# State-space layer: the gate's projection as wide tiles ahead of the loop, products and outputs in twos, tokens weighed ahead of convolutions 4 and 5

## The chip, the cores and the metric

The program runs on one core of a Trainium2 chip. It is a decoder of twelve sublayers on 8 sequences of 128 tokens with 256 channels each; it runs as one launch. The time is device time in microseconds. The kernel before took 2154.83 us (median of three executions, 2151.45 to 2156.3). The change touches the first sublayer alone, a state-space layer that takes about a quarter of the span.

## The reference, cut to what matters

The layer has 32 heads; each has 64 channels of x, 128 of b and 128 of c, and 64 of a gate z. In the reference's terms, for an input of 8 x 128 x 256:

```python
z, x, b, c, dt = split(x @ Win.T)             # per head: 64, 64, 128, 128, 1
x, b, c = (silu(causal_conv(u, w, taps=4)) for u in (x, b, c))
dt  = softplus(dt + dt_bias)
cum = cumsum(-exp(A_log) * dt, over tokens)
y[t] = sum over s <= t of (c[t] . b[s]) * exp(cum[t] - cum[s]) * dt[s] * x[s]
y   = y * silu(z), scaled by the norm of y in each head, then Wout
```

The kernel computes the recurrence as products inside one sequence (128 x 128 for each head and sequence), which is what the sum above says.

## The kernel before, in words

The tokens of all 8 sequences are the free axis (T = 1024), channels are the partitions. `state_space(p)` has three blocks, with a barrier of all engines between them.

The first block (L1702 to L1756) projects dt for all heads on TensorE (L1713), makes softplus and the decays on VectorE (L1732 to L1741), has TensorE sum them over time (L1718), and has VectorE split the sums in three bf16 parts (L1751 to L1756). VectorE also splits the layer's input in a rounded part `XT_hi` and a rest `XT_lo` (L1746, L1747). SyncE starts the load of the next sublayer's weights (L344).

The second block is a loop over 16 pairs of heads, written as a first step, a loop of seven trips with two steps each, and two last steps. One step works on two pairs at once: "a" is the pair whose inputs are projected and convolved, "b" is the pair before it, whose products are made. A pair has five tiles of 128 channels (x, two of b, two of c); I call them 1 to 5, in the code they are 0 to 4.

- Projection of a tile (`project`, L1855): 12 matmuls of 512 columns, in three terms of rounded parts (weights high by input high, high by rest, rest by high) so that the fast 4-byte type keeps the precision. GpSimd makes the two parts of the weights (L1812, L1813). The tiles use two pairs of PSUM banks in turn, so the projection of tile k+2 waits for the convolution of tile k.
- Tap (`tap`, L1960, ScalarE): the last tap of the convolution, from PSUM. Convolution (`convolve`, L2024, VectorE): the three other taps, three dependent instructions. Then `silu` (L1969, ScalarE).
- `turn_x` (L1903, TensorE): tile 1 transposed in two halves; `weigh_x` (L2042, VectorE): each half times dt. They share bank 7.
- For pair b: `decay_sums` (L1866 to L1870, TensorE) and `decay` (L1975, ScalarE, Exp) in four groups; `products` (L1888, TensorE), `mix` (L2034, VectorE: product times decay), `outputs` (L1897, TensorE), each also in four groups, which I call 1 to 4.
- The gate: `project_z` (L1877) makes 16 matmuls of plain float32 with 128 columns each per pair; `silu` of it is L1990; its weights are the last third of the second load of the pair.
- The end of a step: ScalarE copies the outputs (L2002) and squares them (L2004), VectorE sums the squares per head (L2071), GpSimd multiplies by the gate (L1832). The next `decay_sums` wait for the square, since they write the banks that it reads.

Every engine runs its own instructions in the order written. Inside a step the order of these calls in each engine's `step` function is the schedule, and semaphores hold an engine at an instruction until its inputs or its buffer are ready; whatever is written behind waits too. The third block scales, transposes and projects the result.

## Time and profile before

| | us |
|---|---|
| median of three executions | 2154.83 (2151.45 to 2156.3) |
| profiled execution: its own time | 2158.32 |
| profiled execution: its span | 2156.5 |
| TensorE matmul busy, share of the span | 1645.3, 76% |
| VectorE busy | 1434.9, 67% |
| ScalarE busy | 728.7, 34% |
| GpSimd busy | 476.9, 22% |
| mean granted TensorE clock | 0.854 |

The span runs from the first to the last instruction; the execution's own time is 1.82 us longer. PE is TensorE's matmuls, PEld its weight loads, DVE is VectorE, ACT is ScalarE, POOL is GpSimd, SP is SyncE. A granted clock of 1.00 is 2.4 GHz and 0.50 is 1.2 GHz. The trace counts a plain float32 matmul twice (x32 for 16), and its matmul ends are modelled, so that the distance between two starts is a better length than the duration of one. Some matmul records are missing. Times in the rows are from the span's start.

### The profile page before, as it was taken

The numbers are of one execution on the slowest core, as the hardware profiler recorded it, in microseconds if no ns is written. First come the engines' busy times: TensorE is split into PE (matmuls) and PEld (weight loads), VectorE is DVE, ScalarE is ACT, GpSimd is POOL, SyncE is SP. The second block draws the span as 40 slices with busy tenths as digits, with TensorE's granted clock in tenths as the row PEclk, the third lists the DMA queues.
The fourth block names the chain that finished last, engine by engine and source line by source line (L and its number), as shares of the span: only waits on it lengthen the run. The fifth ranks groups of instructions, "written<-read, shape, count | busy, mean of one in ns | idle before, by whom it ended". The sixth has DMA issues, their size and how long they took to land. (4 is left out here: it accounts for less than half of the span.)

```text
span 2156.5 us, 32415 instructions
## 1 busy us (share of the span) xinstructions
PE 1645.3 (76%) x11633; PEld 1226.8 (57%) x11662; DVE 1434.9 (67%) x2376; ACT 728.7 (34%) x1143; POOL 476.9 (22%) x549
## 2 busy tenths in 40 slices
PE   2799999998886888166747458889995988888353
PEld 2687888887773564022446234677764875556221
DVE  3588777877225754899576673554446993677977
ACT  0466556665221441233224111333331002345111
POOL 0233323332000421277112002210001322143000
PEclk9899999999897786588869667999996997999555
DMA  2000000000000000000100002000002210100000
GB/s 106 25 24 21 29 29 29 28 16 23 0 0 21 2 7 32 0 0 0 42 3 2 25 0 100 2 19 1 1 1 64 73 39 27 51 4 2 1 0 20
DMA packets 13206, 46.80 MB, mean 22 GB/s; under 512 B 1715, under 2 KB 2356, under 8 KB 11830
## 3 DMA queue, kind: packets, MB, share of 16 engines
q1 hardware_dynamic: 13110, 45.49, 6.1%
q8 instruction: 64, 1.05, 0.2%
q14 instruction: 32, 0.26, 0.0%
HBM read 44.43 MB, written 1.05 MB: 21 GB/s over the span
## 5 line engine op out<-in xcount | busy, mean ns | idle before, releaser
L2024 DVE SCALAR_TENSOR_TENSOR arena<-psum,arena 128x1016 f32<-128x1016 f32 (+2 forms) x240 | 303.9, 1267 | 100.2 <-ACT arena L1960 94.5
L859 DVE TENSOR_REDUCE limits<-psum 128x4 f32<-128x512 f32 (+2 forms) x256 | 148.3, 620 | 95.2 <-PE psum L719 59.0
L1855 PE MATMUL psum<-ssm_XT_hi,ssm_split 128*128 128x512 f32 x640 | 196.0, 409 | 17.3 <-POOL ssm_split L1813 10.9
L827 ACT ACTIVATE PT<-psum 128x1024 f32<-128x1024 f32 x112 | 108.6, 1021 | 120.5 <-PE psum L750 120.5
L719 PE MATMUL psum<-K,QR 32*128 32x256 f32 (+1 forms) x320 | 125.0, 475 | 26.6 <-POOL K L695 16.4
L1960 ACT ACTIVATE arena<-psum,arena 128x1024 f32<-128x1024 f32 x80 | 89.0, 1112 | 158.3 <-PE psum L1855 158.3
L1855 PEld LDWEIGHTS psum<-ssm_XT_hi,ssm_split 128*128 128x128 f32 x640 | 117.4, 193 | 39.5 <-POOL ssm_split L1813 14.0
L2370 PE MATMUL psum<-expert,x 128*128 128x256 f16 x1024 | 114.7, 277 | 16.8 <-POOL expert L2356 16.8
L1812 POOL TENSOR_TENSOR ssm_split<-arena,const 128x256 fp32r<-128x256 f32 x80 | 58.4, 730 | 291.0 <-DMA arena<-in_ssm_in 164.3
L2508 POOL TENSOR_TENSOR fed<-dtx,b_all 128x1024 f32<-128x1024 f32 x32 | 103.1, 3243 | 77.8 <-ACT b_all L2557 44.3
L2370 PEld LDWEIGHTS psum<-expert,x 128*128 128x128 f16 x1024 | 101.5, 99 | 29.8 <-issue 16.9
L2383 DVE SCALAR_TENSOR_TENSOR acc<-psum,gate_now,acc 128x256 f32<-128x256 f32 x256 | 111.2, 483 | 9.2 <-PE psum L2370 8.3
L2577 DVE TENSOR_TENSOR_SCAN state<-decay,fed 128x1024 f32<-128x1024 f32 x32 | 103.1, 3262 | 6.8 <-POOL fed L2508 5.2
L1855 PE MATMUL psum<-ssm_XT_lo,ssm_split 128*128 128x512 f32 x320 | 101.5, 399 | 0.0
L719 PEld LDWEIGHTS psum<-K,QR 32*128 32x128 f32 x320 | 61.0, 219 | 58.5 <-DVE limits L859 21.2
L2521 PE MATMUL psum<-bc_parts,selector 96*128 96x512 bf16 x64 | 22.2, 479 | 89.3 <-DVE read L2585 56.0
L738 PE MATMUL psum<-Q,KT 32*128 32x256 f32 (+1 forms) x640 | 82.0, 557 | 0.4
L470 PE MATMUL psum<-const,X 128*128 128x128 f32 x176 | 41.2, 396 | 51.2 <-DVE X L514 51.2
L1897 PEld LDWEIGHTS psum<-arena,X 128*128 128x128 f32 x512 | 63.5, 191 | 23.7 <-DVE X L2034 20.8
L1897 PE MATMUL psum<-arena,X 128*128 128x64 f32 x512 | 65.9, 272 | 13.4 <-DVE X L2034 13.4
L601 PE MATMUL psum<-XT,arena 128*128 128x512 f32 x128 | 65.5, 676 | 12.9 <-PEq L885 10.0
L766 PE MATMUL psum<-PT,V 128*32 128x128 f32 x2048 | 72.5, 289 | 2.6 <-DVE O L853 2.6
(415 smaller groups left out, 3691.9 us busy)
## 6 DMA issues: line engine op xcount, KB each, us to landing
arena<-in_ssm_in SPq DMA_DIRECT2D x32, 384.0 KB, 3.1
expert_mask<-in_expert_masks SPq DMA_DIRECT2D x32, 256.0 KB, 2.6
arena<-in_L_xattn SPq DMA_DIRECT2D x1, 5120.0 KB, 15.1
arena<-in_L_ffn SPq DMA_DIRECT2D x1, 2592.0 KB, 9.1
arena<-in_L_xattn SPq DMA_DIRECT2D x2, 1280.0 KB, 5.4
arena<-in_L_attn SPq DMA_DIRECT2D x1, 2272.0 KB
arena<-in_L_ffn SPq DMA_DIRECT2D x1, 2176.0 KB, 8.5
arena<-in_L_xattn SPq DMA_DIRECT2D x1, 1667.0 KB, 6.8
```

The lines of the kernel that those rows point to most:

```text
L719: ins = nc.tensor.matmul(score_bank(r)[:, k * n:(k + 1) * n], QR[group(r), b % 2, c0 + k, :], K1[group(r), b % 2, c0 + k, :, :].rearrange( ...
L738: nc.tensor.matmul(exponents[r][:, k * n:(k + 1) * n], KT[group(r), c0 + k, b * P:(b + 1) * P], Q1[group(r), b % 2, c0 + k, :, :].rearrang ...
L827: nc.scalar.activation(PT[:, u % 2, 2 * k:2 * k + 2, :, :].rearrange("p r h q -> p (r h q)"), p.psum[:, (2 + 2 * k) * 512:(4 + 2 * k) * 51 ...
L859: ins = nc.vector.tensor_reduce(limits[:, u % 2, r, :, k], score_bank(r)[:, :].rearrange("p (h k) -> p h k", h=4)[:, :, lo:hi], AX.X, ALU. ...
L1855: ins = nc.tensor.matmul(bank[tile_bank(r, tile) + half][:, :], w_part(tile, kw, c), x_part(kx, c, slice(half * 512, (half + 1) * 512)), s ...
L1897: ins = nc.tensor.matmul(y_of(b, head), decays[:, g, q * P:(q + 1) * P], dtx[:, 1 - r, b, head * 64:(head + 1) * 64], start=True, stop=True)
L1960: nc.scalar.activation(conv[:, (r + tile) % 2, :], tile_psum(r, tile), ACT.Copy, scale=tap_now[:, r, tile, TAPS - 1:TAPS]).then_inc(s.tap_ ...
L2024: ins = nc.vector.scalar_tensor_tensor(out[:, :, ago:], product[:, :, :P - ago], tap, out[:, :, ago:], ALU.mult, ALU.add)
L2370: ins = nc.tensor.matmul(bank[b][:, :D], x16[:, part, c, b * P:(b + 1) * P], expert[:, r % 2, c, :], start=(part == 0 and c == 0), stop=(p ...
L2383: nc.vector.scalar_tensor_tensor(acc[:, b, :], bank[b][:, :D], gate[:, r % 2, b:b + 1], acc[:, b, :], ALU.mult, ALU.add).then_inc(s.produc ...
L2508: nc.gpsimd.tensor_tensor(fed[:, c, :], dtx[:, c, :], b_all[:, r, :], ALU.mult).then_inc(s.input_ready.up(trips), 1)
L2577: nc.vector.tensor_tensor_scan(state[:, c, :], decay[:, c, :], fed[:, c, :], 0.0, ALU.mult, ALU.add).then_inc(s.state_ready.up(trips), 1)
```

## The change

The gate's projection leaves the loop. Four weight tiles of 512 gate channels (`ssm_z`, 512 KB each) are loaded at the start of the first block; GpSimd splits each in two parts of 128 x 1024; TensorE makes 32 groups of six matmuls with 512 columns (three terms by two halves of the channels, the input's parts as the stationary operand) in four banks in turn, 16 groups before the cumulative sums of the decays and 16 behind; ScalarE puts the Silu of each group into `gated`. The input's split moves to the head of the block, its high part to ScalarE. In the loop the second load of a pair is 256 KB in place of 384 KB and waits for another signal. The order of the step changes on TensorE, ScalarE and VectorE: products, mixes and outputs come in twos, the products have one bank more, and the transposition of tile 1 comes behind outputs 3 and 4.

```diff
@@ first block
-            with nc.Block(no_gpsimd_drain=True) as block:
+            with ExitStack() as first, nc.Block(no_gpsimd_drain=True) as block:
+                z_split = [[first.enter_context(nc.sbuf_tensor(f"ssm_z{r}{k}", [P, T], F32R)) for k in range(2)] for r in range(2)]
+                z_raw = [gated[:, 12 + g, :] for g in range(4)]
+                z_bank = lambda n: bank[4 + n % 4]
                 @block.sync
+                    for g in range(4):
+                        sync.dma_start(z_raw[g].rearrange("p (c n) -> p c n", c=DC), p.dram["ssm_z"][g]).then_inc(s.loaded.up(16), 16)
                     p.load_next(sync)
+                @block.gpsimd
+                    for g in range(4):
+                        if g == 0:
+                            pool.wait_ge(s.loaded.sem, s.loaded.at(63))
+                        if g >= 2:
+                            pool.wait_ge(s.z_psum.sem, s.z_psum.at(8 * (g - 2) + 7))
+                        hi, lo = (a[:, :] for a in z_split[g % 2])
+                        p.pool_chain.then(pool, nc.gpsimd.tensor_tensor(hi..., z_raw[g]..., ones8, ALU.mult))
+                        nc.gpsimd.tensor_tensor(lo, z_raw[g], hi.bitcast(F32), ALU.subtract).then_inc(s.split_ready.up(), 1)
                 @block.tensor
+                    def project_z(g, b):
+                        n = 8 * g + b
+                        if b == 0:
+                            pe.wait_ge(s.split_ready.sem, s.split_ready.at(g))
+                        if n == 0:
+                            pe.wait_ge(s.x_ready.sem, s.x_ready.at(1))
+                        if n >= 4:
+                            pe.wait_ge(s.z_ready.sem, s.z_ready.at(n - 4))
+                        products = [(kw, kx, c) for kw, kx in ((0, 0), (0, 1), (1, 0)) for c in range(DC)]
+                        for kw, kx, c in products:
+                            ins = nc.tensor.matmul(z_bank(n)[:, :], (XT_hi, XT_lo)[kx][:, c, b * P:(b + 1) * P],
+                                                   z_split[g % 2][kw]...[:, c, :], ...)
+                        ins.then_inc(s.z_psum.up(), 1)
                     ...                                  # dt's projection
+                    for n in range(16):
+                        project_z(n // 8, n % 8)
                     pe.wait_ge(s.dt_ready.sem, s.dt_ready.at(0))
                     ...                                  # sums over time
+                    for n in range(16, 32):
+                        project_z(n // 8, n % 8)
                 @block.scalar
+                    nc.scalar.copy(XT_hi[:, :, :], p.XT[:, :, :]).then_inc(s.x_ready.up(), 1)
                     ...
+                    for n in range(32):
+                        g, b = divmod(n, 8)
+                        act.wait_ge(s.z_psum.sem, s.z_psum.at(n))
+                        nc.scalar.activation(gated[:, 4 * g:4 * g + 4, b * P:(b + 1) * P], z_bank(n)..., ACT.Silu).then_inc(s.z_ready.up(), 1)
@@ loop, SyncE and GpSimd
-                                sync.wait_ge(s.z_psum.sem, s.z_psum.at(m + -1))
+                                sync.wait_ge(s.split_ready.sem, s.split_ready.at(m * TILES + -1))
-                            pool.wait_ge(s.z_ready.sem, s.z_ready.at(m + -1))
@@ loop, TensorE
-                product_bank = lambda g: bank[5] if g < 2 else bank[6]
+                product_bank = lambda g: bank[(5, 6, 7, 6)[g]]
-                            pe.wait_ge(s.mixed_ready.sem, s.mixed_ready.at(n + -1))
+                            if g == 3:
+                                pe.wait_ge(s.mixed_ready.sem, s.mixed_ready.at(n + -2))
                             products(0)
-                            pe.wait_ge(weights_here[1].sem, weights_here[1].at(m * 16 + -1))
-                            project_z()
-                            outputs(0)
                             products(1)
                         if has_a:
                             project(m, r, 2)
                         if has_b:
+                            outputs(0)
                             outputs(1)
-                            pe.wait_ge(s.z_ready.sem, s.z_ready.at(m + -1))
                             products(2)
+                            products(3)
                         if has_a:
-                            pe.wait_ge(s.conv_silu.sem, s.conv_silu.at(m * TILES))
-                            turn_x(0)
                             project(m, r, 3)
                         if has_b:
                             outputs(2)
-                            products(3)
+                            outputs(3)
                         if has_a:
+                            pe.wait_ge(s.conv_silu.sem, s.conv_silu.at(m * TILES))
+                            turn_x(0)
+                            project(m, r, 4)
                             pe.wait_ge(s.dtx_ready.sem, s.dtx_ready.at(m * 2))
                             turn_x(1)
-                            project(m, r, 4)
-                        if has_b:
-                            outputs(3)
```

On VectorE, in a step of the loop, the mixes (TENSOR_TENSOR X), the convolutions (three SCALAR_TENSOR_TENSOR) and the two weighings (TENSOR_TENSOR arena, 128x512) stand so before, from mix 2 to the second weighing:

```order
L2034 TENSOR_TENSOR X<-psum,X 128x512
...
L2024 SCALAR_TENSOR_TENSOR arena<-psum,arena 128x8x127
...
L2034 TENSOR_TENSOR X<-psum,X 128x512
...
L2042 TENSOR_TENSOR arena<-psum,arena 128x512
...
L2024 SCALAR_TENSOR_TENSOR arena<-psum,arena 128x8x127
...
L2034 TENSOR_TENSOR X<-psum,X 128x512
...
L2042 TENSOR_TENSOR arena<-psum,arena 128x512
```

and in the changed kernel from mix 2 on (of each convolution the first of its three instructions is shown in both):

```order
L2066 TENSOR_TENSOR X<-psum,X 128x512
...
L2056 SCALAR_TENSOR_TENSOR arena<-psum,arena 128x8x127
...
L2056 SCALAR_TENSOR_TENSOR arena<-psum,arena 128x8x127
...
L2066 TENSOR_TENSOR X<-psum,X 128x512
...
L2066 TENSOR_TENSOR X<-psum,X 128x512
...
L2074 TENSOR_TENSOR arena<-psum,arena 128x512
...
L2056 SCALAR_TENSOR_TENSOR arena<-psum,arena 128x8x127
...
L2074 TENSOR_TENSOR arena<-psum,arena 128x512
```

Mix 2 now stands ahead of convolution 2 and mix 4 ahead of the first weighing; convolutions 2 and 3 stand together.

On TensorE, in the same step, behind outputs 2 (L1897, 128x64), stand products (L1888), the first half of the transposition (L1903, from `sin`) and the projection of tile 4 (L1855) before:

```order
L1897 MATMUL psum<-arena,X 128x64 x4
L1932 REGISTER_ALU
L1888 MATMUL psum<-ssm_bc 128x128 x4
L1903 MATMUL psum<-const,sin 128x128 x4
L1850 REGISTER_ALU
L1855 MATMUL psum<-ssm_XT_hi,ssm_split 128x512 x2
```

and in the changed kernel, from products 3 and 4 (L1929) over the projection of tile 4 (L1903, five rows) to the transposition (L1944) and the projection of tile 5:

```order
L1929 MATMUL psum<-ssm_bc 128x128 x4
L1929 MATMUL psum<-arena,ssm_bc 128x128 x4
...
L1903 MATMUL psum<-ssm_XT_hi,ssm_split 128x512 x2
L1903 MATMUL psum<-ssm_XT_lo,ssm_split 128x512 x2
L1903 MATMUL psum<-ssm_XT_hi,ssm_split 128x512 x4
...
L1938 MATMUL psum<-arena,X 128x64 x8
L1944 MATMUL psum<-const,sin 128x128 x4
...
L1903 MATMUL psum<-ssm_XT_hi,ssm_split 128x512 x2
```

The transposition that the first weighing needs moved from ahead of the projection of tile 4 to behind outputs 3 and 4.

On ScalarE, in the same step, from the first tap behind the Silu of tile 1 on, stand the taps (L1960), the Silus (L1969; L1990 for the gate), the copy (L2002) and the square (L2004) before:

```order
L1960 ACTIVATE arena<-psum,arena 128x1024
...
L1990 ACTIVATE ssm_gated<-psum 128x1024
L1969 ACTIVATE ssm_bc<-arena 128x1024
...
L1960 ACTIVATE arena<-psum,arena 128x1024
...
L1960 ACTIVATE arena<-psum,arena 128x1024
L1969 ACTIVATE ssm_bc<-arena 128x1024
...
L1960 ACTIVATE arena<-psum,arena 128x1024
L1969 ACTIVATE ssm_bc<-arena 128x1024
...
L2002 COPY ctxT<-psum 128x1024
L2004 ACTIVATE cos<-psum 128x1024
```

and in the changed kernel (taps L1996, Silus L2005, copy L2031, square L2033):

```order
L1996 ACTIVATE arena<-psum,arena 128x1024
...
L1996 ACTIVATE arena<-psum,arena 128x1024
L2005 ACTIVATE ssm_bc<-arena 128x1024 x2
...
L1996 ACTIVATE arena<-psum,arena 128x1024
...
L2031 COPY ctxT<-psum 128x1024
L2033 ACTIVATE cos<-psum 128x1024
L2005 ACTIVATE ssm_bc<-arena 128x1024
...
L1996 ACTIVATE arena<-psum,arena 128x1024
```

Tap 5, which stood ahead of the Silu of tile 4, now stands behind it; copy and square moved ahead of both.

## Rows read from the trace of the kernel before

**Rows 1.** Stretch, us, busy us (instructions) of PE, PEld, DVE, ACT, POOL, clock, DMA.

```profile
90.00:506.00 416.00, 394.58 (x2601) 338.68 (x2611) 328.28 (x307) 249.14 (x265) 134.54 (x180) 1.00 0.08 27
...
41.00:45.00 4.00, 3.32 (x16) 3.11 (x16) 3.97 (x6) 0.00 (x0) 0.00 (x0) 1.00 0.00 0
55.30:61.00 5.70, 5.62 (x13) 4.46 (x14) 0.00 (x0) 0.04 (x1) 2.85 (x5) 0.50 0.19 69
```

**Rows 2.** TensorE in order of time, one step: start us, us, engine line op, [idle before].

```profile
238.58 0.38 PE L1867 MATMUL psum<-ssm_cumT,ssm_third 96*128 96x512 bf16 x1 [0.74 <-ACT cos L2004]
...
241.00 0.71 PE L1855 MATMUL psum<-ssm_XT_hi,ssm_split 128*128 128x512 f32 x2
...
243.82 1.12 PE L1888 MATMUL psum<-ssm_bc 128*128 128x128 f32 x8
244.78 3.74 PE L1877 MATMUL psum<-arena,XT 128*128 128x128 f32 x32
248.35 1.00 PE L1897 MATMUL psum<-arena,X 128*128 128x64 f32 x8
249.19 1.11 PE L1888 MATMUL psum<-arena,ssm_bc 128*128 128x128 f32 x8
...
254.66 0.60 PE L1903 MATMUL psum<-const,sin 128*128 128x128 f32 x4
```

**Rows 3.** VectorE in order of time, the same step.

```profile
258.61 0.68 DVE L2042 TENSOR_TENSOR arena<-psum,arena 128x512 f32<-128x512 f32 x1
259.21 3.87 DVE L2024 SCALAR_TENSOR_TENSOR arena<-psum,arena 128x1016 f32<-128x1016 f32 x3
262.99 0.68 DVE L2034 TENSOR_TENSOR X<-psum,X 128x512 f32<-128x512 f32 x1
...
268.97 1.21 DVE L2071 TENSOR_REDUCE arena<-cos 128x1024 f32 x1
```

**Rows 4.** ScalarE in order of time, the same step.

```profile
244.33 1.28 ACT L1969 ACT_TABLE_LOAD   x1 [0.60 <-DVE arena L2024]
...
246.59 1.10 ACT L1960 ACTIVATE arena<-psum,arena 128x1024 f32<-128x1024 f32 x1
...
264.03 1.12 ACT L1960 ACTIVATE arena<-psum,arena 128x1024 f32<-128x1024 f32 x1 [3.92 <-PE psum L1855]
```

**Rows 5.** VectorE in order of time: the sums of squares, first, fifteenth and last.

```profile
119.89 1.21 DVE L2071 TENSOR_REDUCE arena<-cos 128x1024 f32 x1
...
537.45 1.21 DVE L2071 TENSOR_REDUCE arena<-cos 128x16 f32<-128x1024 f32 x1
...
560.05 1.22 DVE L2071 TENSOR_REDUCE arena<-cos 128x16 f32<-128x1024 f32 x1 [3.17 <-ACT cos L2004]
```

**Rows 6.** All engines in order of time, the layer's first block.

```profile
26.25 7.01 PE L1713 MATMUL psum<-arena,XT 128*128 128x32 f32 x32 [0.97 <-PEq L391]
...
41.12 3.32 PE L1718 MATMUL psum<-const,ssm_bc 128*96 128x128 f32 x16 [7.86 <-DVE ssm_bc L1741]
...
49.78 0.68 DVE L1756 CAST ssm_cumT<-ssm_bc 32x1024 bf16<-32x1024 f32 x1
...
55.38 1.22 PE L1855 MATMUL psum<-ssm_XT_hi,ssm_split 128*128 128x512 f32 x2 [10.94 <-POOL ssm_split L1813]
```

**Rows 7.** DMA issues: out<-in engine op xcount, KB each, us to landing.

```profile
arena<-in_L_xattn SPq DMA_DIRECT2D x2, 1280.0 KB, 5.4
...
arena<-in_L_ffn SPq DMA_DIRECT2D x1, 2176.0 KB, 8.5
```

**Rows 8.** GpSimd by line: out<-in xcount | busy us, mean ns | idle before.

```profile
L2508 POOL TENSOR_TENSOR fed<-dtx,b_all 128x1024 f32<-128x1024 f32 x32 | 103.1, 3243 | 77.8 <-ACT b_all L2557 44.3 <-DVE state L2577 33.4
...
L1832 POOL TENSOR_TENSOR ssm_gated<-ctxT,ssm_gated 128x1024 f32 x14 | 33.1, 2363 | 21.8 <-ACT ctxT L2002 21.8
L695 POOL TENSOR_TENSOR K<-KT,const 128x512 fp32r<-128x512 f32 x32 | 32.6, 1040 | 0.0
```

**Rows 9.** ScalarE by line, the same columns.

```profile
L1975 ACT ACTIVATE X<-psum 128x512 f32<-128x512 f32 x64 | 33.2, 604 | 0.5 <-PE psum L1870 0.3
```

More of the change, by code:

```diff
@@ L1683, in state_space @@
             dtx = spare(2, B, P)
-            bc = [[spare(T) if (r, k) == (1, 3) else sb2(f"bc{r}{k}", [P, T])[:, :] for k in range(TILES - 1)] for r in range(2)]
+            early = [sb2(f"bc0{k}", [P, T])[:, :] for k in range(2)]
+            late = spare(T)
             XT_hi = sb2("XT_hi", [P, DC, T], F32R)
@@ L1689, in state_space @@
             third = sb2("third", [P, 2, SSM_H], BF16)
-            dta3 = bc[0][0][:, :B * 3 * SSM_H].rearrange("p (b k h) -> p b k h", b=B, k=3)
-            rest = bc[0][1]
+            dta3 = early[0][:, :B * 3 * SSM_H].rearrange("p (b k h) -> p b k h", b=B, k=3)
+            rest = early[1]
             ones = p.c("ones").rearrange("p (o n) -> p o n", o=1).broadcast_to([P, DC, P])
@@ L1757, in state_space @@
             p.close()
+            bc = [early + [sb2(f"bc0{k}", [P, T])[:, :] for k in (2, 3)], [sb2(f"bc1{k}", [P, T])[:, :] for k in range(3)] + [late]]
             def steps(engine, emit, chain=None, links=0):
@@ L1871, in decay_sums @@
                             ins.then_inc(s.decay_psum.up(trips), 1)
-                        def project_z():
-                            for b in range(B):
-                                for c in range(DC):
-                                    ins = nc.tensor.matmul(bank[6 + b // 4][:, b % 4 * P:(b % 4 + 1) * P], p.XT[:, c, b * P:(b + 1) * P],
-                                                           raw[:, 1, c, 2 * P:], start=(c == 0), stop=(c == DC - 1))
-                            ins.then_inc(s.z_psum.up(trips), 1)
                         def products(g):
                             n = m * 4 + (g - 4)
-                            pe.wait_ge(s.mixed_ready.sem, s.mixed_ready.at(n + -1))
+                            if g == 3:
+                                pe.wait_ge(s.mixed_ready.sem, s.mixed_ready.at(n + -2))
                             for q in range(4):
@@ L2004, in step @@
                             nc.scalar.activation(square[:, :], p.psum[:, 4 * 512:6 * 512], ACT.Square).then_inc(s.square_ready.up(trips), 1)
+                        if has_a:
+                            silu(m, r, 3)
+                            tap(m, r, 4)
                         if has_next:
@@ L2060, in step @@
                             mix(2)
+                            mix(3)
                         if has_a:
@@ L2063, in step @@
                             convolve(m, r, 3)
-                        if has_b:
-                            mix(3)
-                        if has_a:
                             weigh_x(1)
```

45 lines of the change are left out of this document (23 added, 22 removed).

## The prediction, made before the changed kernel ran

> **What bounds the kernel now.** I read the windows first, then one step of the loop engine by engine, then the layer's first block. In the loop TensorE is busy 394.58 of 416 us (95%) and VectorE 328.28 (79%) [rows 1]; the reader is to see that TensorE looks full but that VectorE is not far behind. The sums of squares, one per step, stand 29.83 us apart: (537.45 - 119.89) / 14 [rows 5]. So the loop has one fixed period, and the question is which circle of waits closes in it.
>
> One step, read off starts [rows 2]: the four decay sums take 2.64 (241.00 - 238.58, and 0.22 for their first matmul, whose record is missing), a projection 2.82 (243.82 - 241.00), one group of products 0.96, the gate's projection 3.57 (248.35 - 244.78), one group of outputs 0.84. On VectorE a convolution holds the engine 3.78 and is done after 3.87, a mix or a weighing 0.60 (0.68), the sum of squares 1.13 (270.10 where the next starts; its duration is 1.21) [rows 3]. On ScalarE a tap takes 1.10 to 1.12, the table load and the Silu behind it 2.26 (246.59 - 244.33) [rows 4], so a Silu 0.98.
>
> The circle of before runs over the gate's projection. Decay sums 2.64, projection of tile 2 2.82, products 1 0.96, gate 3.57, outputs 1 0.84, products 2 0.96, projection 3 2.82, then 0.2 until it is seen, tap 3 1.12, convolution 3 3.78, mix 3 0.70, outputs 3 0.84, products 4 0.96, half a transposition 0.36, projection 5 2.82, 0.2, then on ScalarE tap 5, Silu 4, copy and square, about 1.0 + 1.0 + 0.9 + 1.0, and 0.2 until TensorE restarts, which the 0.74 idle before the decay sums shows [rows 2]. The sum is 29.7, against 29.83 measured. This is why I trust such sums to about 0.1 here.
>
> **The change, part by part.**
>
> *The loop loses the gate.* 3.57 us of TensorE and one Silu of 1024 columns per step. If nothing else closed the circle the step would fall to 26.2. But another circle stands just behind, and the new order makes it longer. Follow VectorE through the new step: convolutions 2 and 3 back to back, 7.56; mix 3 until TensorE can start outputs 3, 0.71 (mix 4 runs beside it); outputs 3 and 4, 1.68; the transposition, 0.60 until its end [rows 2]; first weighing 0.60; convolution 4 3.87, with 0.03 until ScalarE sees it; Silu 4 0.98, which now stands ahead of tap 5; tap 5 1.15; convolution 5 3.78; sum of squares 1.13; the next pair's convolution 1 3.90; table load and Silu 1 2.26; tap 2 1.15; and convolution 2 again. The sum: 7.56 + 0.71 + 1.68 + 0.60 + 0.60 + 3.90 + 0.98 + 1.15 + 3.78 + 1.13 + 3.90 + 2.26 + 1.15 = 29.4. Of this 21.6 lie on VectorE; the other 7.8 are three places where its next link is elsewhere: 2.28 for outputs and transposition, 2.13 for Silu 4 and tap 5, 3.41 for table load, Silu 1 and tap 2 (mixes and the second weighing fill part of them). Before, the transposition was ready long before the weighing, and tap 5 stood ahead of Silu 4. Copy and square run early, in the shade of convolution 4, so the old circle is gone; what is late next is VectorE. With the 0.1 by which my sum for before fell short, a step takes 29.45, and 14 periods give 14 x (29.45 - 29.83) = **-5.3**.
>
> *The last step* has no pair a. From the fifteenth sum of squares to the last are 22.6 us [rows 5]. Before, it was products 1, gate, outputs 1, then three rounds in series of products 0.96, 0.2, mix 0.70, outputs 0.84: 0.96 + 3.57 + 0.84 + 3 x 2.7 = 13.5. In twos: products 1 and 2 1.92, 0.2, mix 2 0.70, outputs 2 0.84, products 3 and 4 1.92, 0.2, mix 4 0.70, outputs 4 0.84 = 7.3. **-6.2**. The first step has no pair b and stays.
>
> *The first block grows.* Before, TensorE has 7.01 us of work for dt, waits 7.86, and sums over time in 3.32; VectorE ends the block at 49.78 + 0.68 = 50.46, and the loop's first projection comes at 55.38, 4.92 later, for barrier, load and split [rows 6]. After: the four loads are issued at about 26.2. They are 2048 KB together; between 5.4 us for 1280 KB and 8.5 for 2176 KB [rows 7] that is 8.1, so 34.3. GpSimd then makes two operations on 128 x 1024. That form with two full operands takes 2.36 in one line and 3.24 in another; with a constant operand, 512 columns take 1.04, so 2.08 for 1024 [rows 8]. I take 2.36, the row with the same size beside busy VectorE, and 4.7 for both: the gate's matmuls start at 39.0. The bounds: 33.3, where dt's projection ends, and 34.3 + 6.5 + 5.4 (if the next sublayer's 1280 KB shares the engines) = 46.2. A matmul of this form comes every 2.82 / 12 = 0.235 us, six make 1.41, 32 groups 45.1. The Silu of 512 columns costs about the 0.60 of the Exp of 512 [rows 9], under 1.41, so four banks suffice and TensorE sets the pace. The splits of the third and fourth weight tile take 4.7 beside 8 groups of 11.3: hidden. Softplus (33.3 to 41.1) and the chain behind the sums, which ran alone for 6 us before, are hidden too; ScalarE's and VectorE's input split fits before dt is there. The sums over time stand between the groups with their 3.3. The block's TensorE work ends at 39.0 + 45.1 + 3.3 = 87.4, the last Silu with 0.8 more at 88.2, the first projection at 88.2 + 4.9 = 93.1: **+37.7** against 55.38. It comes because 512 columns in three terms for the whole gate still cost 45 us against 57 in the loop (16 x 3.57), and here only some 12 us of waits stand by to hide them.
>
> *The rest.* The second load of a pair is smaller and asked for earlier, and only GpSimd's split waits for it. No link of either circle waits for GpSimd in the step shown [rows 2]: nothing, and nothing to lose as long as the splits keep ahead of TensorE. The gate's Silu in a step was not on the circle either.
>
> **TensorE's clock.** After the idle 33.3 to 41.1 the sums over time ran at a granted 1.00 (2.4 GHz); after 44.4 to 55.4 the first projections ran at 0.50 (1.2 GHz), until 61.0 [rows 1, 6]. The new idle ahead of the gate, about 6 us, is shorter than the first of these, so I count no slow stretch there; if there is one as long as the 5.6 us of before, it costs 2.8. The loop's start keeps its slow stretch. The Trainium skill, TensorE: Matmul & The Clock Gate, section on HAM oscillation, warns that a wait between bursts brings the slow clock back; by that rule the sum would be 2.8 higher. The sums over time speak against it, the loop's first projections for it.
>
> **Sum.** 37.7 - 5.3 - 6.2 = +26.2 on the profiled execution's 2158.32, or 2184.5 (span 2182.7). Three executions had the median 2154.83; against it I forecast **2181**.
>
> **The rivals.**
>
> *A, TensorE sets the loop's pace, and it falls by the whole 3.57.* For it: 95% busy against 79% [rows 1], and the gate does lie on the circle of before. Against it: the circle over VectorE, whose links are all data or program order. It decides if the step drops below 29.83 - (37.7 - 6.2) / 14 = 27.6. At 26.25 the loop gains 50, the last step 6.2: 2154.8 + 37.7 - 56.2 = 2136, faster. The Trainium skill, Perfetto Trace Analysis, section Identifying the Most-Contended Engine, says to improve the engine with the highest occupancy and to judge TensorE by its weight loads; these are 338.68 of 416, 81%, still above VectorE's 79%, so that rule speaks for this rival.
>
> *B, part of the three waits closes*, because Silu 4 or the transposition finds its input earlier than in my circle, and the step is 28.4: -20 for the loop, 2166.
>
> *C, the new order loses in the loop.* VectorE's handovers cost 0.05 to 0.1 more each (there are eight in the circle) and the step is 30.2: +5 in place of -5, 2191; with a late first load (46.2) or the slow clock, 2194 to 2201.
>
> *D, the first block is not TensorE's.* If GpSimd's 128 x 1024 took over 5.6 us each, or the Silus over 1.41, the block would grow further. No row is near either.
>
> **How the numbers follow.** Forecast 0.70 (2171 to 2191), C and D 0.14, B 0.10, A 0.06. I put the range at 2167 to 2195: it leaves out A and the ends of B and C. This kernel's measurement tells 0.2%, 4.3 us, from no change. A gives faster 0.06; between A and B lies "the same", 0.02; all else is slower, 0.92.
>
> **What would show it.** In the changed kernel's profile: the gate's first matmul near 39 and the last near 87, with the loop's first projection near 93 (the step of the first block); sums of squares 29.4 apart (the circle); VectorE idle ahead of the first weighing until the transposition, about 1.8, ahead of convolution 5 until tap 5, about 1.6, and ahead of convolution 2; TensorE in the loop no longer 95% but about 84% busy; 16 us from the fifteenth sum to the last. A period of 27.6 or less would make the forecast's sign wrong, a first projection before 85 or behind 105 its size.

## The result, and the profile after

The changed kernel takes 2186.11 us (median of four, 2181.52 to 2188.04) against 2153.14 for the kernel before (2149.77 to 2156.3): ratio 1.015, with an interval of 1.0126 to 1.0174. It is slower by 33 us; 2181 was forecast. The profiled execution takes 2188.04 (span 2186.2), 29.7 more than the profiled one of before, where the sum had 26.2.

The layer's first block on TensorE, changed kernel (start us, us, engine line op, [idle before]):

```profile
26.25 7.00 PE L1749 MATMUL psum<-arena,XT 128*128 128x32 f32 x32 [0.97 <-PEq L393]
38.41 1.22 PE L1742 MATMUL psum<-ssm_z,ssm_XT_hi 128*128 128x512 f32 x2 [5.15 <-POOL ssm_z L1728]
...
63.45 1.91 PE L1756 MATMUL psum<-const,ssm_bc 128*96 128x128 f32 x16
...
87.04 0.62 PE L1742 MATMUL psum<-ssm_z,ssm_XT_hi 128*128 128x512 f32 x2
...
93.36 1.22 PE L1903 MATMUL psum<-ssm_XT_hi,ssm_split 128*128 128x512 f32 x2 [5.70 <-POOL ssm_split L1862]
```

They answer to [rows 6]. The gate's matmuls run from 38.41 to 87.66 with the sums over time between them, and the loop's first projection stands at 93.36 in place of 55.38.

The sums of squares, first, fifteenth and last, which answer to [rows 5]:

```profile
155.02 1.21 DVE L2099 TENSOR_REDUCE arena<-cos 128x1024 f32 x1
...
573.48 1.21 DVE L2099 TENSOR_REDUCE arena<-cos 128x16 f32<-128x1024 f32 x1
590.13 1.22 DVE L2099 TENSOR_REDUCE arena<-cos 128x16 f32<-128x1024 f32 x1 [3.17 <-ACT cos L2033]
```

They cut the layer in four pieces:

| piece, us | before | after | difference | predicted |
|---|---|---|---|---|
| until the loop's first projection | 55.38 | 93.36 | +38.0 | +37.7 |
| from there to the first sum | 64.51 | 61.66 | -2.85 | 0 |
| 14 periods | 14 x 29.83 | 14 x 29.89 | +0.9 | -5.3 |
| fifteenth to last sum | 22.60 | 16.65 | -5.95 | -6.2 |
| until the last sum | 560.05 | 590.13 | +30.1 | +26.2 |

The loop's windows (stretch, us, busy of PE, PEld, DVE, ACT, POOL, clock, DMA), beside [rows 1]:

```profile
93.30:155.00 61.70, 50.50 (x258) 39.03 (x260) 42.61 (x38) 27.72 (x28) 21.66 (x32) 0.93 0.09 27
...
120.00:540.00 420.00, 365.76 (x2179) 297.35 (x2194) 331.79 (x308) 241.58 (x254) 136.47 (x181) 0.98 0.07 22
```

TensorE fell from 95% busy to 365.76 of 420, 87%, VectorE stayed at 79%: 3.57 us of matmuls left each step and nothing was gained by it. The granted clock was 0.98, where it had been 1.00.

VectorE in a step whose outputs and transposition ran at full clock, from mixes 3 and 4 to convolution 5, and TensorE beside it:

```profile
320.88 1.28 DVE L2066 TENSOR_TENSOR X<-psum,X 128x512 f32<-128x512 f32 x2
324.18 0.69 DVE L2074 TENSOR_TENSOR arena<-psum,arena 128x512 f32<-128x512 f32 x1 [2.02 <-PE psum L1944]
...
330.79 3.88 DVE L2056 SCALAR_TENSOR_TENSOR arena<-psum,arena 128x1016 f32<-128x1016 f32 x3 [1.23 <-ACT arena L1996]
```

```profile
321.62 2.00 PE L1938 MATMUL psum<-arena,X 128*128 128x64 f32 x16 [1.01 <-DVE X L2066]
323.45 0.60 PE L1944 MATMUL psum<-const,sin 128*128 128x128 f32 x4
```

The three gaps of the new circle are there: 2.02 ahead of the first weighing (1.8 was forecast), 1.53 ahead of convolution 5 in most steps (1.6; 1.23 in this one, where the clock fell to 0.50 at 323.9, behind the transposition, and the second weighing came later), 1.10 to 1.15 ahead of convolution 2. From the start of mix 3 to the weighing are 3.30 (324.18 - 320.88); the circle had counted 0.71 + 1.68 + 0.60 = 2.99.

In some steps TensorE's clock falls to 0.50 soon after its wait for mix 3. Two windows of one, then TensorE and VectorE in it:

```profile
291.40:294.00 2.60, 2.60 (x21) 2.60 (x21) 0.54 (x1) 1.90 (x3) 0.49 (x1) 0.85 0.00 0
294.00:296.00 2.00, 2.00 (x7) 1.61 (x6) 1.58 (x2) 1.49 (x2) 0.00 (x0) 0.50 0.00 0
```

```profile
291.40 2.04 PE L1938 MATMUL psum<-arena,X 128*128 128x64 f32 x16 [1.13 <-DVE X L2066]
293.24 1.06 PE L1944 MATMUL psum<-const,sin 128*128 128x128 f32 x4
```

```profile
294.42 0.69 DVE L2074 TENSOR_TENSOR arena<-psum,arena 128x512 f32<-128x512 f32 x1 [2.48 <-PE psum L1944]
```

The transposition takes 1.06 in place of 0.60, the weighing waits 2.48 in place of 2.02, and the step is 30.26 long (304.82 - 274.56) where its neighbours are 29.76. The periods are, in order, 30.21, 29.76, 29.81, 29.76, 30.26, 29.76, 29.81, 29.76, 30.36, 29.97, 29.80, 29.77, 29.80, 29.63: the ten undisturbed ones have the mean 29.77, the other four are 1.7 longer together. The clock fell in one more step, the one at 323.9 above; there it met the projection behind the transposition and the step stayed at 29.76. All five slow stretches begin 1.7 to 2.3 behind the end of the wait for mix 3. The steps hold other waits of TensorE too, 1.45 ahead of products 1 among them, so that it is this wait which brings the slow clock is not shown.

### The profile page after: what moved, and what is told of

Its sections match the earlier page's. It is cut to its first block and busy times, and to the rows that moved or that the text cites. A ratio compares the mean times of both kernels' runs of the same rounds, so it can differ in the third digit from the quotient of the medians.

```text
span 2186.2 us, 31711 instructions
## 1 busy us (share of the span) xinstructions
PE 1646.8 (75%) x11313; PEld 1206.7 (55%) x11342; DVE 1443.9 (66%) x2375; ACT 735.3 (34%) x1159; POOL 496.2 (23%) x557
## 5 line engine op out<-in xcount | busy, mean ns | idle before, releaser
L1903 PE MATMUL psum<-ssm_XT_hi,ssm_split 128*128 128x512 f32 x640 | 200.4, 416 | 31.7 <-DVE arena L2056 26.0
L1903 PEld LDWEIGHTS psum<-ssm_XT_hi,ssm_split 128*128 128x128 f32 x640 | 119.4, 197 | 61.6 <-DVE arena L2056 24.0
L2398 PEld LDWEIGHTS psum<-expert,x 128*128 128x128 f16 x1024 | 101.5, 99 | 29.7 <-issue 16.8
L2005 ACT ACTIVATE ssm_bc<-arena 128x1024 f32<-128x1024 f32 x56 | 59.4, 1061 | 135.6 <-DVE arena L2056 135.6
L1996 ACT ACTIVATE arena<-psum,arena 128x1024 f32<-128x1024 f32 x80 | 88.4, 1104 | 44.6 <-PE psum L1903 44.6
L1903 PE MATMUL psum<-ssm_XT_lo,ssm_split 128*128 128x512 f32 x320 | 103.2, 405 | 0.0
```

The source lines that it names most:

```text
L1903: ins = nc.tensor.matmul(bank[tile_bank(r, tile) + half][:, :], w_part(tile, kw, c), x_part(kx, c, slice(half * 512, (half + 1) * 512)), s ...
L1996: nc.scalar.activation(conv[:, (r + tile) % 2, :], tile_psum(r, tile), ACT.Copy, scale=tap_now[:, r, tile, TAPS - 1:TAPS]).then_inc(s.tap_ ...
L2398: ins = nc.tensor.matmul(bank[b][:, :D], x16[:, part, c, b * P:(b + 1) * P], expert[:, r % 2, c, :], start=(part == 0 and c == 0), stop=(p ...
```

## The experiments

My theory: the new loop is paced by the circle over VectorE, and each of its three gaps, taken away, shortens the step; with all of them gone the 3.57 that TensorE was relieved of appear. The main rival: TensorE is the bound and the new order only adds to its work or waits. Each kernel is compared with runs of the kernel before on its own chip.

**Tap 5 first.** The changed kernel, with tap 5 ahead of Silu 4 on ScalarE.

```diff
                         if has_a:
-                            silu(m, r, 3)
                             tap(m, r, 4)
+                            silu(m, r, 3)
```

> The changed kernel with one swap on ScalarE: tap 5 ahead of Silu 4. My theory (the step is closed by a circle over VectorE, whose second gap is Silu 4 and tap 5): the circle loses Silu 4 and TensorE's tap comes as soon as projection 5 is done, 1.6 us per step; sums of squares 28.2 apart in place of 29.9, the whole 2160. Rival (TensorE or its slow clock after the wait for mix 3 sets the step): swapping two ScalarE operations changes nothing, 29.9 apart, 2186.

Measured: 2158.51 (2153.94 to 2161.22), ratio 1.0019, interval 1.0001 to 1.0036; period (544.98 - 150.57) / 14 = 28.17. VectorE, both weighings and convolutions 4 and 5:

```profile
311.14 0.69 DVE L2074 TENSOR_TENSOR arena<-psum,arena 128x512 f32<-128x512 f32 x1 [2.02 <-PE psum L1944]
311.74 3.86 DVE L2056 SCALAR_TENSOR_TENSOR arena<-psum,arena 128x1016 f32<-128x1016 f32 x3
315.52 0.68 DVE L2074 TENSOR_TENSOR arena<-psum,arena 128x512 f32<-128x512 f32 x1
316.12 3.86 DVE L2056 SCALAR_TENSOR_TENSOR arena<-psum,arena 128x1016 f32<-128x1016 f32 x3
```

The gap ahead of convolution 5 is gone, the one ahead of the weighing is as it was, and the step is 1.72 shorter. Two lines of ScalarE, exchanged, are worth nearly 28 us of time (2158.51 against 2186.11, two medians of different chips); in the profiled executions 24 of it lie in the 14 periods and 3.9 ahead of the first sum (57.79 from the first projection, in place of 61.66).

**Tap 2 first.** The same for the third gap: tap 2 ahead of the table load and Silu 1.

```diff
-                            silu(m, r, 0)
                             tap(m, r, 1)
+                            silu(m, r, 0)
                             tap(m, r, 2)
```

> The changed kernel with tap 2 ahead of Silu 1, so ahead of the table load too. My theory: the third gap of the circle (table load, Silu 1, tap 2, 3.4 us) shrinks, until another link closes it; 1.05 us per step, 28.8 apart, 2168. Rival (TensorE or its clock sets the step): nothing, 2186.

Measured: 2165.56 (2162.63 to 2167.15), 1.0051, interval 1.0031 to 1.007; period (554.17 - 154.35) / 14 = 28.56, so 1.33 less. VectorE, mix 2, then convolutions 2 and 3:

```profile
303.85 0.69 DVE L2066 TENSOR_TENSOR X<-psum,X 128x512 f32<-128x512 f32 x1 [0.20 <-PE psum L1929]
304.46 7.64 DVE L2056 SCALAR_TENSOR_TENSOR arena<-psum,arena 128x1016 f32<-128x1016 f32 x6
```

No wait is left ahead of convolution 2.

**Transposition early.** It stands behind the projection of tile 3 again, ahead of that of tile 4; the products give up the third bank for it.

```diff
-                product_bank = lambda g: bank[(5, 6, 7, 6)[g]]
+                product_bank = lambda g: bank[(5, 6, 5, 6)[g]]
...
-                            if g == 3:
+                            if g >= 2:
...
                         if has_a:
+                            pe.wait_ge(s.conv_silu.sem, s.conv_silu.at(m * TILES))
+                            turn_x(0)
                             project(m, r, 3)
```

> The changed kernel with the first transposition back ahead of the projection of tile 4, products 3 in bank 5 in place of bank 7 to make room for it. My theory: the first gap (outputs 3 and 4, transposition, 2.3 us, with VectorE idle 2.0 to 2.5 ahead of the first weighing) goes; 1.35 us per step, 28.5 apart, 2165. If TensorE's slow clock behind that wait is what makes 29.9 out of 29.4, another 0.4 per step comes back, 2159. Rival (TensorE's total work sets the step): the same work, 2186.

Measured: 2155.72 (2153.9 to 2157.76), 1.0014, interval 1.0 to 1.0028; period (546.95 - 153.81) / 14 = 28.08, 1.81 less, near the lower of the two forecasts. VectorE:

```profile
310.30 1.28 DVE L2065 TENSOR_TENSOR X<-psum,X 128x512 f32<-128x512 f32 x2
311.50 0.68 DVE L2073 TENSOR_TENSOR arena<-psum,arena 128x512 f32<-128x512 f32 x1
312.51 3.87 DVE L2055 SCALAR_TENSOR_TENSOR arena<-psum,arena 128x1016 f32<-128x1016 f32 x3 [0.33 <-ACT arena L1995]
...
318.52 3.87 DVE L2055 SCALAR_TENSOR_TENSOR arena<-psum,arena 128x1016 f32<-128x1016 f32 x3 [1.49 <-ACT arena L1995]
```

The weighing follows the mixes at once; 0.33 of the 2.02 come back as a wait for tap 4, and the gap ahead of convolution 5 stays. So 1.69 of the 1.81 is the gap itself, for which 1.35 was forecast, and only the 0.12 left is the slow clock, for which 0.4 was: the total came near the lower forecast for another reason than it gives. Over 120 to 490 the granted clock is 1.00 here, 0.98 in the changed kernel.

**The old order.** The changed kernel with the gate ahead of the loop, but on TensorE, ScalarE and VectorE the order of the kernel before.

```diff
-                product_bank = lambda g: bank[(5, 6, 7, 6)[g]]
+                product_bank = lambda g: bank[5] if g < 2 else bank[6]
...
-                            if g == 3:
-                                pe.wait_ge(s.mixed_ready.sem, s.mixed_ready.at(n + -2))
+                            pe.wait_ge(s.mixed_ready.sem, s.mixed_ready.at(n + -1))
...
```

> The gate's projection ahead of the loop alone: the changed kernel with before's order, banks and waits in the loop, without the gate. My theory: circles of VectorE alone close before's order at 29.1 to 29.2 (before, 29.83): the gate's 3.57 us of TensorE work were worth 0.7 per step; last step 17.7 + about 2 at the slow clock. The whole about 2184, as the changed kernel or a few us less; so the new order as such brought nothing. Rival A (TensorE sets before's loop): 26.3 per step, 2136.

Measured: 2188.29 (2185.86 to 2189.68), 1.0162, interval 1.0128 to 1.0196; period (569.99 - 156.77) / 14 = 29.52. TensorE's outputs 1 to 3 in a step:

```profile
311.04 1.10 PE L1937 MATMUL psum<-arena,X 128*128 128x64 f32 x8 [0.78 <-DVE X L2062]
...
317.51 1.10 PE L1937 MATMUL psum<-arena,X 128*128 128x64 f32 x8 [1.67 <-DVE X L2062]
...
323.51 1.10 PE L1937 MATMUL psum<-arena,X 128*128 128x64 f32 x8 [0.74 <-DVE X L2062]
```

The gate's 3.57 us leave TensorE and 0.31 leaves the step. Three waits for mixes stand here, 3.19 together, where the same step of [rows 2] has only one, of 0.74 ahead of outputs 3; so 2.45 of the 3.57 came back as waits. The last 0.8 would be restarts behind them, since outputs take 0.94 there (318.45 - 317.51) and not 0.84, and the granted clock of 0.98; these were not measured one by one. Rival A (26.3, 2136) falls. So with neither of these two orders does moving the gate pay, and the changed order as a whole loses 0.37 per period against the old one (29.89 against 29.52) but gains 7.4 in the last step (16.65 against 24.04).

**Half the gate left in the loop.** The kernel before, with half of the gate's matmuls left out (one half of the channels is not summed). It asks the same of the kernel before itself: what is TensorE's time there worth?

```diff
-                                for c in range(DC):
+                                for c in range(1):
...
-                                                           raw[:, 1, c, 2 * P:], start=(c == 0), stop=(c == DC - 1))
+                                                           raw[:, 1, c, 2 * P:], start=(c == 0), stop=(c == 0))
```

> The kernel before with half of the gate's products left out (8 matmuls in place of 16 per step, 1.79 us of TensorE less; the output lacks that part of the gate). Theory: before's loop is closed by two circles 0.6 apart; the one over the gate shortens until the one over VectorE closes it at 29.1 to 29.2, 2143. Rival A (TensorE alone sets the pace): 28.0 apart, 2126.

Measured: 2140.04 (2136.99 to 2142.67), 0.9942, interval 0.9926 to 0.9959; period (526.48 - 116.80) / 14 = 29.26. One step's outputs 2 and 3, and the window:

```profile
305.47 1.10 PE L1897 MATMUL psum<-arena,X 128*128 128x64 f32 x8 [0.97 <-DVE X L2034]
...
311.47 1.10 PE L1897 MATMUL psum<-arena,X 128*128 128x64 f32 x8 [0.78 <-DVE X L2034]
```

```profile
120.00:490.00 370.00, 338.97 (x2167) 284.01 (x2178) 297.85 (x278) 221.97 (x239) 123.22 (x164) 1.00 0.09 28
```

1.79 us less of matmuls shortens the step by 0.57. Most of the rest, 0.97, turns into a wait for mix 2 (the one for mix 3 stood there before, with 0.74). TensorE is 92% busy (338.97 of 370), so a second circle over VectorE's mixes stands right behind the first.

**The loop reordered.** The gate ahead as in the change, the step in an order meant to open every gap at once: taps 2 and 5 ahead of the Silus, the transposition early, and each group of outputs one projection later than its mix.

```diff
-                product_bank = lambda g: bank[(5, 6, 7, 6)[g]]
+                product_bank = lambda g: bank[(5, 6, 5, 6)[g]]
...
-                            if g == 3:
+                            if g >= 2:
...
                             project(m, r, 2)
                         if has_b:
+                            products(2)
+                        if has_a:
+                            pe.wait_ge(s.conv_silu.sem, s.conv_silu.at(m * TILES))
+                            turn_x(0)
+                            project(m, r, 3)
+                        if has_b:
                             outputs(0)
+                            products(3)
                             outputs(1)
-                            products(2)
-                            products(3)
                         if has_a:
-                            project(m, r, 3)
+                            project(m, r, 4)
+                            pe.wait_ge(s.dtx_ready.sem, s.dtx_ready.at(m * 2))
+                            turn_x(1)
                         if has_b:
                             outputs(2)
                             outputs(3)
...
+                            tap(m, r, 1)
                             act.wait_ge(s.cb_psum.sem, s.cb_psum.at(m * 4 + -5))
                             silu(m, r, 0)
-                            tap(m, r, 1)
                             tap(m, r, 2)
                             silu(m, r, 1)
+                            tap(m, r, 3)
                             silu(m, r, 2)
-                            tap(m, r, 3)
+                            tap(m, r, 4)
+                            silu(m, r, 3)
...
                         if has_b:
                             mix(0)
-                            mix(1)
                         if has_a:
                             convolve(m, r, 1)
+                        if has_b:
+                            mix(1)
+                            mix(2)
+                        if has_a:
+                            weigh_x(0)
                             convolve(m, r, 2)
                         if has_b:
-                            mix(2)
                             mix(3)
                         if has_a:
-                            weigh_x(0)
                             convolve(m, r, 3)
...
```

> The changed kernel's first block with a loop order laid out so that no gap of VectorE's circle is left: tap 2 ahead of Silu 1, tap 5 ahead of Silu 4, the first transposition ahead of projection 4, products 3 in bank 5, outputs later. My theory: what the gate's 3.57 us of TensorE left behind was hidden by the order alone; sums of squares 24.8 to 25.0 apart, near TensorE's own work per step (24.7), the loop 75 us shorter than the changed kernel's and some us of slow clock less; the whole 2105 to 2112, below both kernels. Rival (the three gaps overlap with something that the single swaps did not show, such as TensorE's clock or GpSimd's splits): the single swaps' gains 1.7, 1.3 and 1.8 don't add, 27 or more apart, 2145.

Measured: 2106.61 (2106.38 to 2108.51), 0.9786, interval 0.977 to 0.9802; period (495.65 - 146.88) / 14 = 24.91. VectorE, one step, and the window:

```profile
302.48 0.69 DVE L2063 TENSOR_TENSOR X<-psum,X 128x512 f32<-128x512 f32 x1 [1.18 <-PE psum L1929]
303.09 3.87 DVE L2053 SCALAR_TENSOR_TENSOR arena<-psum,arena 128x1016 f32<-128x1016 f32 x3
306.87 1.28 DVE L2063 TENSOR_TENSOR X<-psum,X 128x512 f32<-128x512 f32 x2
308.07 0.68 DVE L2071 TENSOR_TENSOR arena<-psum,arena 128x512 f32<-128x512 f32 x1
308.67 3.86 DVE L2053 SCALAR_TENSOR_TENSOR arena<-psum,arena 128x1016 f32<-128x1016 f32 x3
```

```profile
120.00:490.00 370.00, 366.80 (x2300) 307.69 (x2314) 346.19 (x326) 252.74 (x266) 141.85 (x187) 1.00 0.08 25
```

VectorE has one gap of 1.18 in this step and none from there to its sum of squares at 321.21, TensorE is 99% busy at a clock of 1.00: now TensorE is the bound, and the whole is below the kernel before. The step is 4.98 shorter than the changed kernel's; the three single swaps had 1.72 + 1.33 + 1.81 = 4.86, so their gains add.

**The gate in the loop, reordered.** The kernel before with the same cure of the order. It separates the order from the gate's move.

```diff
-                            pe.wait_ge(s.mixed_ready.sem, s.mixed_ready.at(n + -1))
+                            if g % 2:
+                                pe.wait_ge(s.mixed_ready.sem, s.mixed_ready.at(n + -1))
...
                             project_z()
-                            outputs(0)
-                            products(1)
                         if has_a:
                             project(m, r, 2)
...
+                            turn_x(0)
                         if has_b:
-                            outputs(1)
...
+                            products(1)
...
                             products(2)
...
+                            tap(m, r, 1)
                             act.wait_ge(s.cb_psum.sem, s.cb_psum.at(m * 4 + -5))
                             silu(m, r, 0)
-                            tap(m, r, 1)
...
                             convolve(m, r, 1)
+                            weigh_x(0)
                         if has_b:
                             mix(1)
+                            mix(2)
...
```

> The kernel before, its gate left in the loop, with the same cures in the order (tap 2 ahead of Silu 1, first transposition and first weighing early, products 2 and 3 together). Theory: with the order cured the step is TensorE's work, 28.3; 28.4 to 28.5 apart, the loop 29 us shorter, 2125. Against the reordered loop with the gate ahead it then shows what moving the gate is worth: 50 in the loop for 38 ahead of it. Rival (the order cures are only worth something with the gate gone): 29.8 apart, 2154.

Measured: 2127.96 (2122.0 to 2141.12), 0.9892, interval 0.9849 to 0.9935; period (513.05 - 111.99) / 14 = 28.65. The window:

```profile
120.00:490.00 370.00, 367.10 (x2412) 313.74 (x2424) 308.69 (x285) 233.27 (x245) 128.63 (x169) 1.00 0.08 28
```

TensorE is full here too (367.10 of 370). The order alone is worth 24 us (2127.96 against 2151.83) and takes 1.18 off each period. Between two loops that TensorE fills, the gate's move is worth 28.65 - 24.91 = 3.74 per step, the 3.57 and a little more: 52 in 14 periods, for 38 ahead of the loop, and 21 us of time (2106.61 against 2127.96). The two loops are alike in their cures, not line by line. Between two loops that it doesn't fill the move was worth 0.3 per step.

**Two terms of the gate.** The changed kernel with the third term of the gate's product (low part of the weights by high part of the input) left out.

```diff
-                        products = [(kw, kx, c) for kw, kx in ((0, 0), (0, 1), (1, 0)) for c in range(DC)]
+                        products = [(kw, kx, c) for kw, kx in ((0, 0), (0, 1)) for c in range(DC)]
```

> The changed kernel with the gate's third term left out (four matmuls in place of six in each of the 32 groups; the gate is less exact). Theory of the first block: TensorE sets its pace at 0.235 us a matmul, 64 less are 15.0 us, 2171, with the loop untouched. Rival (GpSimd's splits, 4.8 us a weight tile, or the Silus, 0.60 a group, set it): less than 3 us.

Measured: 2170.28 (2167.67 to 2175.64), 1.0087, interval 1.0067 to 1.0107. The loop's first projection:

```profile
78.67 1.22 PE L1903 MATMUL psum<-ssm_XT_hi,ssm_split 128*128 128x512 f32 x2 [5.85 <-POOL ssm_split L1862]
```

That is 14.7 earlier than 93.36 for 64 matmuls fewer, 0.23 each: TensorE sets the first block's pace (against rival D). The period is 29.82, as it was.

**The first weight tile alone.** The loop reordered, where GpSimd's first split waits for the first of the four loads alone.

```diff
-                        sync.dma_start(...).then_inc(s.loaded.up(16), 16)
+                        sync.dma_start(...).then_inc((s.weights0 if g == 0 else s.loaded).up(16), 16)
...
                         if g == 0:
-                            pool.wait_ge(s.loaded.sem, s.loaded.at(63))
+                            pool.wait_ge(s.weights0.sem, s.weights0.at(15))
+                        if g == 1:
+                            pool.wait_ge(s.loaded.sem, s.loaded.at(47))
```

> loop_reordered with one edit in the first block: the split of the first gate tile waits for its own load and not for all four. Theory: the gate's first matmul moves from 38.4 to 39.7 back to about 34 or 35, since the first 512 KB are there some 4 us before the fourth; TensorE sets the block's pace, so the whole gets 4 us shorter, 2102 against 2106. Rival (the four loads share the DMA engines and land together): nothing, or under 1 us.

Measured: 2103.58 (2100.58 to 2107.17), 0.9763, interval 0.9741 to 0.9785. GpSimd's first split and the gate's first matmul:

```profile
29.95 2.76 POOL L1729 TENSOR_TENSOR ssm_z<-ssm_gated,const 128x1024 fp32r<-128x1024 f32 x1 [29.50 <-DMA ssm_gated<-in_ssm_z]
```

```profile
35.25 1.22 PE L1744 MATMUL psum<-ssm_z,ssm_XT_hi 128*128 128x512 f32 x2 [4.02 <-POOL ssm_z L1730]
```

The matmul stands 4.4 earlier than in the loop reordered (39.66), the loop's first projection 4.7 (89.33 against 94.07). In the ratio the intervals of the two overlap, so the 3 us are shown in the trace but not by the times. It is the fastest version measured, 2.4% under the kernel before.

## Why the prediction was right, step by step

*The mechanism of the loop was right.* The circle over VectorE with its three gaps paces the new step: taking away any one gap, with TensorE's work as it was, shortened it (by 1.72, 1.33 and 1.81); in the old order, 3.57 us less of TensorE's work gave only 0.31; and rival A took place only when the order was changed (24.91, TensorE 99%).

*The term for 14 periods was mis-sized, and its sign was wrong:* "a step takes 29.45 ... -5.3" measured 29.89 and +0.9. (Its own terms, 29.40 and the 0.1, add up to 29.5, which gives -4.6.) Of the 0.44 per step, 0.32 are in undisturbed steps (29.77), and 0.31 of these lie in one piece, the 3.30 from the start of mix 3 to the weighing, counted as 2.99. I took outputs and transposition from a TensorE that never stopped ([rows 2]); behind a wait, outputs 3 and 4 take 1.83 (323.45 - 321.62) in place of 1.68 and the transposition 0.73 until VectorE starts. The other 0.12 is the slow clock from the transposition on: 1.7 in four steps. I looked for the clock at the gate and the loop's start only, and not at the waits that I was putting into the loop myself. Rival C had the step at 30.2; the truth lies between it and the forecast.

*The last step* was -5.95 for -6.2.

*Between the first projection and the first sum* 2.85 were gained that no term had. That stretch holds the first step, without a pair b, and the second, which has the gate's projection before and not after. I counted 14 periods and the last step and left this step out. TensorE's busy time in the stretch falls from 53.35 (55.3 to 120) to 50.50, also by 2.85, but that is not the cause by itself: the old order without the gate needs 63.24 there (156.77 - 93.53), 1.27 less than before, and the other 1.58 came with the new order. That these are single executions with slow stretches of their own leaves the shares rough. The gain offsets half of the miss in the periods, and that it does is luck.

*The first block* was +38.0 for +37.7, out of errors that cancel; so near a hit is luck too. The loads landed by 33.52 (34.3 was forecast), GpSimd's two operations took 2.34 and 2.41 (2.36 each), so the gate began at 38.41 (39.0). The sums over time took 1.67 between two groups (65.12 - 63.45), not 3.3: the 3.32 of before is the same 16 records at half the rate, as the last section shows. Against that a group comes every 1.40 (44.32 to 45.72, and on), but the first two took 2.56 and 2.34 (39.42 to 41.98 to 44.32), at half the rate: some 2.5 more in all, with the 0.46 of the first pair (1.01 for 0.55), which the forecast had put at nothing. Behind the block 5.7 pass until the first projection; the sum had the same, 0.8 for the last Silu and 4.9.

The Trainium skill, TensorE: Matmul & The Clock Gate, section on HAM oscillation, had said that a wait between bursts brings the slow clock back. The forecast weighed it against the sums over time of before and took zero for 2.8. Here the rule was right at the gate's start (2.5). And the row that was held against it was misread: the sums of before follow an idle of 7.86 and took 3.32, the changed kernel's follow a busy TensorE and took 1.91 by the same measure, so the sums too ran slow behind their wait. In the loop slow stretches came as well, 1.7 to 2.3 behind a wait of 1.0 to 1.1; the section's own case is a longer wait for a load, so these are a finding of the runs.

The Trainium skill, Perfetto Trace Analysis, section Identifying the Most-Contended Engine, would have had TensorE optimized first. The runs show what that is worth by itself in this loop: 3.57 us less for 0.31 per step with the old order. With the gaps opened first, the same 3.57 gave 3.74, and there TensorE, 99% busy, was the engine to relieve.

## What to carry to other kernels

An engine that is 95% busy may still have a second circle of waits 0.3 us behind it, so read the period as a circle, link by link, for the old order and for the new, before you take work off the busiest engine. Open the gaps first (in one case by exchanging two lines of an engine that is 34% busy), then move the work: the same move cost 34 us with the old order (2188.29 against 2154.07) and gave 21 with the gaps open (2106.61 against 2127.96); the order alone gave 24. And each wait that a new order gives to TensorE is to be priced with its restart and with a slower clock behind it, and a count of steps is to include the first and second.

## What the runs showed of the hardware

**Some VectorE operations stand still while GpSimd works.** VectorE in the first block of the changed kernel, GpSimd beside it, and VectorE in the kernel before:

```profile
33.75 2.40 DVE L1782 SCALAR_TENSOR_TENSOR arena<-arena 128x256 f32<-128x256 f32 x1
36.63 1.87 DVE L2663 TENSOR_SCALAR arena<-arena 128x256 f32<-128x256 f32 x1 [0.48 <-ACT arena L1767]
38.53 8.22 DVE L2665 SCALAR_TENSOR_TENSOR arena<-arena 128x256 f32<-128x256 f32 x9
```

```profile
33.52 2.34 POOL L1727 TENSOR_TENSOR ssm_z<-ssm_gated,const 128x1024 fp32r<-128x1024 f32 x1 [33.07 <-DMA ssm_gated<-in_ssm_z]
35.94 2.41 POOL L1728 TENSOR_TENSOR ssm_z<-ssm_gated,ssm_z 128x1024 fp32r<-128x1024 f32 x1
38.31 2.42 POOL L1727 TENSOR_TENSOR ssm_z<-ssm_gated,const 128x1024 fp32r<-128x1024 f32 x1
40.81 2.44 POOL L1728 TENSOR_TENSOR ssm_z<-ssm_gated,ssm_z 128x1024 fp32r<-128x1024 f32 x1
```

```profile
33.75 0.43 DVE L1734 SCALAR_TENSOR_TENSOR arena<-arena 128x256 f32<-128x256 f32 x1
34.66 0.29 DVE L2635 TENSOR_SCALAR arena<-arena 128x256 f32<-128x256 f32 x1 [0.48 <-ACT arena L1726]
34.99 4.10 DVE L2637 SCALAR_TENSOR_TENSOR arena<-arena 128x256 f32<-128x256 f32 x9
```

An operation of 0.43 becomes one of 2.40, one of 0.29 becomes 1.87, and their ends, 36.15 and 38.50, come 0.29 and 0.15 behind the ends of GpSimd's operations, 35.86 and 38.35. The nine take 4.1 more than before, and all of it lies in the first two: they take 2.48 and 2.49, the other seven 0.42 to 0.43, and GpSimd's fourth operation ends at 43.25. So VectorE's operation does not run slower, it waits for the other to end. The page SBUF — State Buffer of the Trainium skill, section SBUF: two separate sides, calls the port pair that the two engines share an exclusive lock held for a whole instruction, where VectorE's operation has two SBUF inputs or runs in a two-port mode; these rows agree. It cost nothing here, since the sums over time that need the chain stand 16 groups later; with the softplus on the path it would have cost some 7.7 (1.97 + 1.58 + 4.12).

**A granted clock of 1.00 can stand for no record.** Between 38.4 and 44 the changed kernel's window names a granted clock of 1.00, while 13 matmul records fill 5.59 us, 0.43 each; in the kernel with tap 5 first the same matmuls with the same durations stand at 0.50 up to 42. The changed kernel's trace holds no record of the clock before 44.05, that of the kernel before none before 43.89, and the windows give 1.00 there.

```profile
38.40:44.00 5.60, 5.59 (x13) 4.43 (x14) 5.49 (x4) 0.67 (x2) 4.78 (x2) 1.00 0.00 0
```

So the 1.00 at 41 to 45 in [rows 1], on which the prediction put the sums over time at full speed, says little. The kernel with half of the gate has the same first block, and there the record exists:

```profile
38.90 3.73 PE L1718 MATMUL psum<-const,ssm_bc 128*96 128x128 f32 x16 [7.87 <-DVE ssm_bc L1741]
```

```profile
38.40:44.00 5.60, 3.73 (x16) 3.38 (x16) 5.34 (x9) 0.00 (x0) 0.00 (x0) 0.50 0.00 0
```

The 16 records take 3.73 at 0.50, 3.32 in the kernel before (0.42 each, but 0.27 for the last three, behind 43.89) and 1.91 in the changed kernel at a recorded 1.00. The durations are the surer sign of the two levels (2.4 and 1.2 GHz).
